# A hybrid attention, state-space and expert block: fp32 spread of B, second state by products, masks and expert products on GpSimd

## The reference, cut to what matters

```python
x = x + conv(group_norm(x), Wq, Wk, Wv)      # attention over 1024 pixels, per image
t = tokens(x)                                 # 4 images, 1024 tokens, 128 channels
t = t + mamba_both_ways(layer_norm(t))        # inner residual included
t = t + moe(layer_norm(t))                    # 8 experts, best 2 of each token
# attention keeps the 102 largest scores of each row
topk_vals, topk_idx = jax.lax.top_k(scores, 102)
attn = softmax(scores where kept, else -inf)
# mamba, forward and on the flipped sequence: 256 channels, 16 states
xs = silu(conv4(xz)); dbc = xs @ x_proj_w.T
dt = softplus(dbc[:, :16] @ dt_proj_w.T + dt_proj_b)
h[s] = exp(dt * A[s]) * h_prev[s] + dt * B[:, s] * xs      # scan over 1024 tokens
y = sum_s h[s] * C[:, s] + xs * D
# experts
out = tokens + sum_e combine[:, e] * (gelu(tokens @ w1[e] + b1[e]) @ w2[e] + b2[e])
```

## Time and profile before

| | |
|---|---|
| time, median of 3 runs | 1713.32 us (1710.85 to 1717.54) |
| the profiled execution | 1710.06 us, its span 1708.3 us |
| VectorE busy | 1351.4 us, 79% of the span |
| TensorE busy | 1287.6 us, 75%; granted clock 0.884 on average |
| ScalarE, GpSimd busy | 986.3 us (58%), 784.2 us (46%) |
| the DMA rows | 75.17 MB moved, 44 GB/s |

### The profile page before, as it was taken

How to read it: one execution, slowest core, us unless ns; L and a number is a source line. 1 busy time by engine, 2 the same in 40 slices (tenths; PEclk the granted TensorE clock), 3 DMA queues, 4 the chain that set the end, 5 groups by cost and what they waited for, 6 DMA issues and landing times. The chain is left out here.

```text
span 1708.3 us, 18307 instructions
## 1 busy us (share of the span) xinstructions
PE 1287.6 (75%) x4658; PEld 673.2 (39%) x4658; DVE 1351.4 (79%) x1579; ACT 986.3 (58%) x1366; POOL 784.2 (46%) x426
## 2 busy tenths in 40 slices
PE   3308688888577778888846878888857777898868
PEld 2106253433435344343422625343343534344444
DVE  2785889897797679989688588989779767998942
ACT  1705777674724586677452577767473458766713
POOL 3002468686100538878210256878610053786830
PEclk8658789999788879999969878999978886999989
DMA  2000012221000012222000011222200001222200
GB/s 67 0 1 1 28 50 98 74 98 62 1 1 13 2 39 86 99 74 98 15 0 1 14 28 49 97 75 96 66 1 1 13 2 39 86 87 86 86 13 13
DMA packets 25842, 75.17 MB, mean 44 GB/s; under 512 B 4246, under 2 KB 8220, under 8 KB 25756
## 3 DMA queue, kind: packets, MB, share of 16 engines
q1 hardware_dynamic: 25756, 74.19, 12.6%
HBM read 71.56 MB, written 2.62 MB: 43 GB/s over the span
## 5 line engine op out<-in xcount | busy, mean ns | idle before, releaser
L589 POOL TENSOR_TENSOR work<-expo,ring 128x1024 f32<-128x1024 f32 x128 | 299.8, 2363 | 131.8 <-DVE expo L1193 125.6
L589 POOL TENSOR_TENSOR ring<-ring 128x1024 f32<-128x1024 f32 x128 | 299.9, 2366 | 34.9 <-DVE ring L1193 34.9
L1193 DVE TENSOR_TENSOR_SCAN ring<-ring,ps 128x1024 f32<-128x1024 f32 x128 | 284.3, 2262 | 36.6 <-ACT ring L816 36.6
L1606 PE MATMUL ps<-ring,ident 128*128 128x512 f32 x512 | 265.3, 623 | 31.8 <-POOL ring L589 21.8
L1193 DVE TENSOR_TENSOR_SCAN expo<-ring,ps 128x1024 f32<-128x1024 f32 x128 | 285.6, 2271 | 4.1 <-ACT ring L816 4.1
L1606 PE MATMUL ps<-work,ident 128*128 128x512 f32 x512 | 241.1, 593 | 0.0
L619 ACT ACTIVATE b_dtx_tok<-dtx_tok,b_tok 128x256 f32<-128x256 f32 x512 | 215.7, 493 | 0.3
L816 ACT ACTIVATE ring<-dt_f,decay 128x1024 f32<-128x1024 f32 x128 | 146.3, 1149 | 99.2 <-DVE expo L1193 61.3
L547 POOL TENSOR_TENSOR ln_rstd<-ln_var,neg_half 128x4 f32<-128x4 f32 x8 | 11.9, 1492 | 375.2 <-DVE ln_var L1090 375.2
L1572 PE MATMUL ps<-ident,b_dtx_tok 128*128 128x128 f32 x1024 | 137.8, 279 | 52.6 <-DVE expo L1193 41.7
L1572 PEld LDWEIGHTS ps<-ident,b_dtx_tok 128*128 128x128 f32 x1024 | 109.7, 140 | 151.6 <-issue 79.8
(11 more groups left out here) (272 smaller groups left out, 2224.9 us busy)
## 6 DMA issues: line engine op xcount, KB each, us to landing
ring<-c_rows SPq DMA_DIRECT2D x128, 512.0 KB, 3.6
x_c<-in_x SPq DMA_DIRECT2D x4, 512.0 KB, 4.2
out<-xs_f SPq DMA_DIRECT2D x4, 512.0 KB, 2.9
w<-in_L_ffn_w SPq DMA_DIRECT2D x2, 512.0 KB
ring<-in_L_attn_f_in_proj_w SPq DMA_DIRECT2D x1, 256.0 KB
ring<-in_L_attn_b_in_proj_w SPq DMA_DIRECT2D x1, 256.0 KB
c_rows<-dbc_f SPq DMA_DIRECT2D x4, 64.0 KB, 1.9
c_rows<-xh SPq DMA_DIRECT2D x4, 64.0 KB, 1.9
```

Of the source, the lines that this page charges most:

```text
L589: pool.tensor_tensor(hc[odd][:, k, :], hs[odd][:, k, :], c_all[:, odd, :], ALU.mult).then_inc(hc_ready, 1)
L1193: v.tensor_tensor_scan(hs[odd][:, k, order], dA[:, k, order], dbu[:, order], 0.0, ALU.mult, ALU.add).then_inc(scan_ready, 1)
L1606: last = mm(halves(ps[2 * k])[h], ident[:, :], hc[odd][:, k, h * BANK:(h + 1) * BANK], start=False, stop=stop)
```

## The change

Eleven edits, all in one kernel:

1. The bf16 parts of B are gone (`rest`, `last_part`, `middle_part`, two copies). `pick` is fp32 and has 16 rows; the spread is an fp32 matmul of the 16 rows of B.
2. State 1 of a direction is no longer weighed and turned back: it has a spread and two products of its own (`second_state`). A direction has 9 spreads instead of 8, and 7 turn-backs of two blocks instead of 8. In the backward direction the two PSUM tiles swap roles.
3. A table set that holds exp and log is loaded once ahead of the softplus.
4. The logs of the backward direction stand behind the first two decays; the first scans of the forward direction stand around the two `dt_sum` of the backward one.
5. The last count writes its 0/1 (VectorE) or sign (ScalarE) result as bf16 (`below`); it waits for `thresh`, not only for `neg_thresh`.
6. GpSimd multiplies scores and `below` (`mask_scores`) into four buffers, two of them `expo`; `max` waits for it. The exponents wait until the search is done.
7. GpSimd makes the expert products (`select`), between the masks.
8. Their weights go through DRAM: 8 rows are stored, and each is loaded spread over 128 partitions, two in turn (`load_weights`).
9. The combine weights have no bf16 parts either.
10. `resolve` has one more small operation.
11. TensorE's loop over the pairs is unrolled.

```diff
@@ SyncE
+            def load_weights(m):
+                sp.wait_ge(comb_copied, m + 1)
+                sp.dma_start(comb_rows[:, :], comb_t).then_inc(comb_stored, 16)
+                sp.wait_ge(comb_stored, 16 * (m + 1))
+                passed(sp)
+                for x in range(EXPERTS):
+                    sp.wait_ge(sel_ready, m * EXPERTS + max(x - 1, 0))
+                    sp.dma_start(weight_rows[x % 2],
+                                 comb_rows[x:x + 1, :].to_broadcast([P, N])).then_inc(weight_loaded[x % 2], 16)
...
                 load_image(b)
+                load_weights(b - 1)
                 store_image(b - 1)
@@ GpSimd
+            def mask_scores(b, m=None):
+                for j in range(TILES):
+                    if m is not None and j >= 2:
+                        select(m, j - 2)
+                    if j < ACT_TILES:
+                        pool.wait_ge(counted, ((b + 1) * COUNTS - 1) * ACT_TILES + j + 1)
+                    else:
+                        pool.wait_ge(ranked, b + 1)
+                    pool.wait_ge(laddered, b * TILES + max(j - 3, 0))
+                    pool.tensor_tensor(low_scores[j % 4], score[:, j, :], below[j], ALU.mult).then_inc(masked, 1)
+                if m is not None:
+                    select(m, EXPERTS - 2)
+                    select(m, EXPERTS - 1)
+            def select(m, x):
+                n = m * EXPERTS + x
+                pool.wait_ge(weight_loaded[x % 2], 8 * EXPERTS * m + 16 * (x // 2 + 1))
+                pool.wait_ge(gelu_ready, n + 1)
+                pool.wait_ge(expert_added, m * EXPERTS + max(x - 1, 0))
+                pool.tensor_tensor(sel_e[:, x % 2, :], act_e[:, x % 2, :], weight_rows[x % 2],
+                                   ALU.mult).then_inc(sel_ready, 1)
...
                 if m is not None:
                     expert_norm(m)
+                mask_scores(b, m)
                 layer_norm(b)
@@ ScalarE
             def exponent(b, i):
                 act.wait_ge(neg_max_ready, b + 1)
+                act.wait_ge(laddered, (b + 1) * TILES)
...
                 conv_tanh(b, 1, 1)
+                nc.scalar.preload_act_table_set("natural_log_exp_and_others")
                 dt_log(b, 0, 0)
                 b_and_c(b, 1)
                 dt_log(b, 0, 1)
                 dt_abs(b, 1, 0)
-                middle_part(b, 1)
                 dt_abs(b, 1, 1)
-                dt_log(b, 1, 0)
-                dt_log(b, 1, 1)
...
+                decay_of(0, 0, first=True)
+                decay_of(0, 1, first=True)
+                if d == 0:
+                    dt_log(b, 1, 0)
+                    dt_log(b, 1, 1)
...
+                to_tokens(0)
+                decay_of(1, 0)
+                to_tokens(1)
+                decay_of(1, 1)
@@ VectorE
-                    step(v.scalar_tensor_tensor(work[:, j % 2, :], score[:, j, :], thresh[:, j:j + 1],
-                                                score[:, j, :], ALU.is_lt, ALU.mult))
+                    dve.wait_ge(masked, b * TILES + j + 1)
+                    passed(dve)
+                    step(v.max(ladder[:, j, 1:9], low_scores[j % 4]))
...
+                link(v.scalar_tensor_tensor(found[:, :], thresh[:, :], 0.0, found[:, :], ALU.is_gt, ALU.mult))
...
+            def second_state(b, d):
+                products(b, d, 1, 1, 1 - d)
+                for k in range(BLOCKS):
+                    scan_product(b, d, 1, 1, 1, 1 - d, k, first=d == 0)
...
-                products(b, 0, 0, 0, first=True)
+                products(b, 0, 0, 0, 0, first=True)
+                dve.wait_ge(gate_ready, b * DIRS * BLOCKS + 1)
+                scan_product(b, 0, 0, 0, 0, 0, 0, first=True)
                 dt_sum(b, 1, 0)
+                scan_product(b, 0, 0, 0, 0, 0, 1, first=True)
                 dt_sum(b, 1, 1)
...
-                for j in range(0, TILES, 2):
-                    first_below((j, j + 1))
-                    if m is not None:
-                        select(m, j)
-                    next_below((j, j + 1))
-                    if m is not None:
-                        select(m, j + 1)
+                for j in range(0, TILES, 2):
+                    first_below(b, (j, j + 1))
+                    next_below(b, (j, j + 1))
@@ TensorE
-                pe.wait_ge(scan_ready, base if first and d == 0 else base + 4 * r - 1)
+                pe.wait_ge(scan_ready, base if first and d == 0 else base + 2 * s - 1)
                 for h in range(HALVES):
-                    last = mm(halves(state_in[turn])[h], pick[:, ds(2 * r, 1), :].rearrange("p o m -> p (o m)"),
-                              bc_parts[d][:, h * BANK:(h + 1) * BANK], start=True, stop=True)
+                    last = mm(halves(state_in[turn])[h], pick[:, s, :],
+                              dbc[d][0:D_STATE, h * BANK:(h + 1) * BANK], start=True, stop=True)
```

More of the change, by code:

```diff
@@ L613, in _ @@
             expert_norm(BATCH - 1)
+            for x in range(EXPERTS):
+                select(BATCH - 1, x)
         @block.scalar
@@ L1194, in scan, with scan_product, scan_turned @@
                                      ALU.mult, ALU.add).then_inc(scan_ready, 1)
[L1196 to L1198 removed]
+            def scan_product(b, d, s, odd, n, turn, k, first=False):
+                spreads = (b * DIRS + d) * SPREADS
+                scan(b, d, s, odd, turn, k, (dbu_ready, 2 * (spreads + n) + k + 1), first)
+            def scan_turned(b, d, r, turn, k):
+                pairs = (b * DIRS + d) * (PAIRS - 1)
+                scan(b, d, 2 * r + 1, 1, turn, k, (turned_back, 2 * (pairs + r - 1) + k + 1))
             def apply_gate(b, d, k):
```

273 lines of the change are left out of this document (107 added, 166 removed).

## The result

The changed kernel takes 1688.07 us (median of 4 runs, 1685.88 to 1697.71), the kernel before 1712.18 on the same chip (4 runs, 1710.85 to 1717.54). The ratio is 0.986, 95% interval 0.982 to 0.991: faster by 1.4%. The profiled execution has a span of 1684.2 us against 1708.3, so there are 24.1 us to explain.

The account below looks back on a forecast made before the run. VectorE was taken to bound the state loop and search, no engine all stages. From 1710.06 us, -9.3 - 18 - 8 - 4 + 15.6 - 4.5 = -28.2 gave 1681.9, named as 1683; range 1660 to 1701.

Parts of the forecast that it names:

- Search, image 0: Search of the first image: VectorE's masking moves to GpSimd, one small operation in resolve is added; -9.3 us.
- Search, images 1 to 3: Search of later images: GpSimd's masks and expert products, waiting for the weights, set the end; -6.1 us each, -18 in all.
- Preparation: Preparing the forward states, up to the first pair's products: -2 us an image, -8 in all, bounds +4 and -36.
- What is late next is TensorE: Preparation of the forward states: with ScalarE and VectorE relieved, TensorE's matmuls, partly at half clock, set the first products.
- State loop: Loop over pairs of states: the longer fp32 spread costs 0.30 us a pair at 52 spreads, +15.6; bounds nothing and +66.
- 9.56 + 1.99: State loop: spread starts 9.56 us behind the products, next products 1.99 after that: 11.55 a pair, where VectorE needs 11.25.
- Start of the backward states: Start of the backward direction: the second state's two products fill VectorE's wait; -1 us an image, -4 in all.
- After the last image: Stretch behind the fourth image: expert products on GpSimd, then TensorE's matmul pairs, end sooner; -4.5 us, bounds -6 and 0.
- The rival of the clock: State loop: TensorE's clock falls because spreads use 16 rows; 1.7 us per pair hit, 1771 if all 52; chance 0.08.

Follow-up runs that it names:

- e3: The changed kernel with GpSimd's masks 2 and 3 ahead of expert products 0 and 1 in images 1 to 3: 1680.11 us, ratio 0.981.
- e11: e9 with GpSimd's masks 2 to 4 held until the combine weights are made, then run ahead of expert product 0: 1610.32 us, ratio 0.939.
- e1: The changed kernel with the fp32 spread on all 128 rows instead of 16, the added weights zero: 1663.25 us, ratio 0.969.
- e9: e8 with the dt matmuls, too, on all 128 rows, weights zero outside the 16 rows of dt: 1625.47 us, ratio 0.948.
- e13: e9 without the one load of the common table ahead of the softplus, so eight loads an image: 1648.22 us, ratio 0.962.
- e8: The changed kernel with the 128-row spread of e1 and another TensorE order in each pair, turn-backs and spread issued earlier: 1648.40 us, ratio 0.962.
- e2: The changed kernel with TensorE's spread moved half an add forward in each pair: 1687.47 us, ratio 0.984.
- e14: The kernel before with its dt matmuls on 128 rows, weights zero outside the 16 of dt: 1710.86 us, ratio 0.999.
- e5: The changed kernel with the bf16 parts and the 96-row bf16 spread put back: 1642.75 us, ratio 0.960.
- e12: e11's GpSimd order and 128-row dt matmuls, with the bf16 parts and spreads of e5 and the changed kernel's TensorE order: 1626.43 us, ratio 0.948.

## Why the prediction was right, and where it was not

The time (1683 against 1688.07) was right, by errors that partly cancel.

- **Search, image 0.** Right but for 1.8: the copy behind the mask. The section that I weighed for max and strike, of the Trainium skill, "SBUF — State Buffer", Who interferes with whom, names the copy too, and I didn't go through the other operations of the stage with it.
- **Search, images 1 to 3.** The mechanism is shown in the rows: the wait of the first expert product, 8.7 us behind the combine weights (forecast 8.8), then GpSimd without a gap. It gained 8.1 and not 6.1 an image, for the twelve operations from product 0 to mask 7 took 26.4 and not 28.3: a mask takes 2.13, and I had taken the price of the fp32 operation. e3 and e11 confirm that GpSimd's order holds the masks.
- **Preparation.** -13.1 against -8. "What is late next is TensorE" holds: e1 and e9 shorten it by TensorE alone. Image 0 (-6.0) and image 1 (+0.3) differ in its clock: from 77 us behind the start of resolve on, it is low for 21 us in the one and for 31 in the other. e13 points to ScalarE as next behind it.
- **State loop, the term that failed.** 0.58 a pair and not 0.30, +28.3 and not +15.6. The mechanism (9.56 + 1.99, in place of the VectorE bound of 11.25) was right and the size was not: 0.19 are for 16 rows between matmuls of 128 (e1), 0.1 for the distance to VectorE, which I took from another consumer. That the chain and not TensorE's load set it is shown by e8, and by the 27 pairs of e2 at full clock.
- **Start of the backward states.** -1.1 against -4: behind the second products VectorE waits 1.76 for the spread of the first pair, which the fp32 price made late.
- **After the last image.** -4.2 against -4.5.
- **The rival of the clock.** It didn't fall in the loop of the changed kernel: 1.00 there. It did in e2, in 21 of 48 pairs, where it cost 1.1 to 1.2 us each and not the 1.7 that I had worked out. That the forecast escaped it is partly luck, for the loop of e2 differs by half an add. Few rows in use, the reason that I gave for it, bear on the clock in the preparation, by e1 and e9: from the changed kernel to e9 it went from 111.8 to 102.5 an image, some of it by the order and by shorter spreads. I had given the half clock there as a bound of the term and not seen that the change's own spreads prolong it.
- **Scores.** -2.1 in all, unforecast, and nearly all of it the 1.9 of image 0. Its largest score comes at 53.1 to 53.3 us in the profiles in which the granted clock rises at 36.4 to 37.2, and at 55.1 to 55.7 in those in which it rises at 41.4 to 42.6: the kernel before, e14, e5, e12 and both without the table load. So it is the clock; why it rises later in these stays open.

What the forecast did not see at all: the fp32 spread and GpSimd's order had a better form. Price by part, in us: the fp32 spread as made +45 (e5), the one table load -23 in e9's surroundings (e13), the search with GpSimd's masks and products -32 (by the marks).

## What to carry to other kernels

When an operation in a loop gets longer, look first at its place in its engine's order: here 0.4 us a pair came back by issuing it one add earlier and the turn-backs ahead of adds. When a move gives nothing, look at the granted clock of each turn of the loop before you blame the order: in e2 the mean hid pairs at full clock that had the whole gain. Small matmuls filled with zero weights up to 128 rows, next to others as wide, gave 24 and 23 us in the changed kernel and nothing in the kernel before, where another engine was late. Before work goes to GpSimd, list every VectorE operation that will run beside it by its SBUF inputs and kind, the tiny ones in dependent chains above all.

## What the runs showed of the hardware

- The granted clock was 0.50 over 18.6 us in which TensorE had no gap, with matmuls of 16 rows among them; with the spreads on 128 rows it rose for good 10 us sooner (e1), and beside the dt matmuls, on 128 rows too, it was 0.97 (e9).
- In a loop in which TensorE was busy for 43.5 of 44 us, with 16-row spreads, the clock fell to 0.50 for 3.4 us in 21 of 48 pairs, and each such pair was 1.1 to 1.2 us longer (e2).
- The scores of image 0 took 1.9 us longer in profiles in which the clock rose 5 us later, with the instructions ahead of them at the same times.
- An fp32 matmul pair of 512 columns on 16 rows between such of 128 rows takes 1.91 to the next start, and the matmul ahead of it 1.81, where 128 rows take 1.72 each.
- A VectorE copy of 128x8 fp32 numbers took 0.17 alone and 2.10 beside a GpSimd product; tensor_scalar of 128x4 0.16 and 2.07.
- GpSimd's product of 128x1024 took 2.34 with two fp32 inputs and 2.13 with one in bf16.
